# Own tiles transposed once and rescaled by a row on VectorE; the other tiles' statistics as running sums on ScalarE

## The reference

```python
xn = (x - mean) / sqrt(var + 1e-5)
# attention branch, per channel a decaying sum over earlier tokens
xm  = xn * time_mix + shift_one_token(xn) * (1 - time_mix)
k   = exp(min(xm @ Wk.T, 60));  v = xm @ Wv.T;  r = xm @ Wr.T
out1 = (sigmoid(r) * decaying_sum(k * v) / (decaying_sum(k) + 1e-16)) @ Wo.T
# ffn branch: a second normalisation of xn, then a ternary matrix
z   = (xn - mean(xn)) * rsqrt(var(xn) + 1e-3) * gamma + beta
g   = max(abs(z))                 # over the whole input
out2 = clip(z * 128 / g, -128 + 1e-5, 128 - 1e-5) @ ternary(W) * scale(g)
y = x + out1 + out2
```

## Time and profile before

| | us |
|---|---|
| median of 3 runs (892.36 to 892.97) | 892.81 |
| profiled execution, its own time | 891.49 |
| span of its trace | 889.7 |
| PE busy in the span | 867.1 (97%) |
| DVE busy | 764.8 (86%) |
| ACT busy | 510.3 (57%) |
| POOL busy | 215.2 (24%) |

### The profile page before, as it was taken

The page is one execution under the profiler, slowest core; times in us unless marked ns, Lnnn a source line. Parts: engine busy times, 40 slices in busy tenths (PEclk is TensorE's granted clock), DMA queues, the critical chain, the costliest instruction groups (busy, mean ns, idle before and its releaser), DMA issues.

```text
span 889.7 us, 12792 instructions
## 1 busy us (share of the span) xinstructions
PE 867.1 (97%) x3984; PEld 714.5 (80%) x3984; DVE 764.8 (86%) x1278; ACT 510.3 (57%) x834; POOL 215.2 (24%) x242
## 2 busy tenths in 40 slices
PE   3989999999999999999999999999999999999998
PEld 2778888888888888888888888888888888888886
DVE  5998999989897999989897897878978888789684
ACT  5584767667594757566564554545546536365441
POOL 5552326242452425240030100200201103011000
PEclk9999999999999999999999999999999999999999
DMA  8222415041423224045643245324451443424311
GB/s 283 108 83 88 149 54 184 13 171 54 165 71 135 101 82 154 12 172 136 212 145 115 84 154 189 125 75 141 153 175 57 157 141 96 154 93 142 95 48 47
DMA packets 59841, 107.13 MB, mean 120 GB/s; under 512 B 7712, under 2 KB 7712, under 8 KB 59808
## 3 DMA queue, kind: packets, MB, share of 16 engines
q1 hardware_dynamic: 59808, 106.73, 35.1%
HBM read 64.76 MB, written 41.96 MB: 120 GB/s over the span
## 4 chain that ended last, share of the span: by engine, by line
PE 90%; DVE 3%; issue 2%; POOL 2%; ACT 1%; DMA 0%; SPq 0%; POOLq 0%; DVEq 0%; ACTq 0%
PE kvr L513 18%; PE kvr L515 18%; PE kvr L514 18%; PE out_banks L552 7%; PE out_banks L554 7%; PE out_banks L534 6%; PE out_banks L533 6%; PE out_banks L531 6%; PE transposed L466 2%; PE out_banks L466 2%; DVE bn_stats L842 1%; POOL normed L1174 1%; POOL own_stats L1156 1%; POOL own_stats L1157 1%; DMA x<-in_x 0%
## 5 line engine op out<-in xcount | busy, mean ns | idle before, releaser
L1247 POOL TENSOR_TENSOR evacuated<-normed,mix_over_ffn_row 128x512 f32<-128x512 f32 x28 | 49.0, 1751 | 339.0 <-DVE ffn_lo L922 339.0
L513 PE MATMUL kvr<-xm_hi,wk_hi 128*128 128x512 f32 x256 | 103.7, 405 | 2.6 <-DVE xm_lo L922 2.6
L513 PE MATMUL kvr<-xm_hi,wv_hi 128*128 128x512 f32 x256 | 102.9, 402 | 2.2 <-DVE wv_lo L927 1.3
L513 PE MATMUL kvr<-xm_hi,wr_hi 128*128 128x512 f32 x256 | 102.7, 401 | 0.0
L515 PE MATMUL kvr<-xm_hi,wk_lo 128*128 128x512 f32 x256 | 101.0, 395 | 0.0
L514 PE MATMUL kvr<-xm_lo,wk_hi 128*128 128x512 f32 x256 | 100.7, 394 | 0.0
L515 PE MATMUL kvr<-xm_hi,wv_lo 128*128 128x512 f32 x256 | 100.2, 391 | 0.0
L515 PE MATMUL kvr<-xm_hi,wr_lo 128*128 128x512 f32 x256 | 100.1, 391 | 0.0
L531 PE MATMUL out_banks<-wo_hi,rwkv_hi 128*128 128x512 f32 x256 | 100.0, 390 | 0.0
L534 PE MATMUL out_banks<-wo_hi,rwkv_lo 128*128 128x512 f32 x256 | 99.7, 389 | 0.0
L514 PE MATMUL kvr<-xm_lo,wr_hi 128*128 128x512 f32 x256 | 99.7, 389 | 0.0
(11 more groups left out here) (140 smaller groups left out, 1922.7 us busy)
## 6 DMA issues: line engine op xcount, KB each, us to landing
other<-ffn_input SPq DMA_DIRECT2D x64, 256.0 KB, 5.1
x<-in_x SPq DMA_DIRECT2D x15, 1024.0 KB, 5.8
other<-in_x SPq DMA_DIRECT2D x8, 1024.0 KB, 5.8
ffn_input<-evacuated SPq DMA_DIRECT2D x32, 256.0 KB, 4.4
ffn_input<-parked SPq DMA_DIRECT2D x32, 256.0 KB, 2.2
attn_scratch<-x SPq DMA_DIRECT2D x8, 1024.0 KB, 4.2
parked<-attn_scratch SPq DMA_DIRECT2D x8, 1024.0 KB, 6.7
out<-parked SPq DMA_DIRECT2D x8, 1024.0 KB, 5.2
```

The source lines that it names most:

```text
L513: nc.tensor.matmul(KVR[:, m, :], hi, XH[t][:, ch, :], start=(ch == 0), stop=False)
L1247: G.tensor_tensor(U[:, n % RING, :], XN[:, ch, :], BC[:, :], ALU.mult).then_inc(pool_v, 1)
```

## The change

- **Own tiles.** Slots ffn_own0 and ffn_own1 become virtual: PE transposes nothing for them. When ACT evacuates a mix slot it first copies the transposed chunk as it is into a new buffer Y. The second normalisation differs from the first only by a factor per token, rsqrt(var(xn) + 1e-3). POOL computes this factor for the 512 tokens (`ratio`, 128x4); PE spreads it by four transposes of a broadcast column into a row that is equal in all partitions (`ratio_row`, after groups 9 and 21, and once at the start); ACT copies that to `RROW`; DVE multiplies the chunk of Y by it (`own_ffn_input`: in groups 10, 11 and twice in 12 for own1, and four after the last low part of a batch for the next own0). ACT then evacuates the virtual slot from Y instead of PSUM.
- **Own normalisations.** ACT's and POOL's second normalisation of own tiles goes, and with it two small POOL steps of nine.
- **Other tiles.** Except for the first one, mean and variance no longer come from bn_stats. ACT makes them as sums: for each of four 128-token blocks an Identity and a Square activation of (x - first channel) with an accumulated output (`other_sums`), after rwkv_hi of chunk 3 in group 12, and after the last high parts of a batch. POOL turns the sums into the variance with five more small operations.
- **Banks and waits.** The first four transposes go to OUT instead of TB and KVR; the wait for attn banks in `slot` moves from slots 1 and 14 to 5 and 16.

```diff
+ROW_AFTER = {9: 1, 21: 0}
...
+            def ratio_row(k, t, bank):
+
+
+                pe.wait_ge(pool_ratio, k + 1)
+                for q in range(Q):
+                    last = nc.tensor.transpose(bank[:, q * P:(q + 1) * P],
+                                               ratio[:, t, q:q + 1].to_broadcast([P, P]), ident[:, :])
+                last.then_inc(pe_row, 1)
...
-                    if ph == "B":
+                    if ph == "B" or n is not None and is_virtual(n):
                         n = None
...
+                    if ph == "A" and g in ROW_AFTER:
+                        t = ROW_AFTER[g]
+                        pe.wait_ge(dve_out, bank_use(b, ph, f"attn{1 - t}") + 1)
+                        ratio_row(2 * b + 2 - t, t, OUT[:, 0, :])
...
+                virtual = ph == "A" and is_virtual(n)
+                if virtual:
+                    act.wait_ge(dve_z, virtual_before(b, n) + 1)
...
+                        nc.scalar.activation(Y[:, ch, :], bank, ACT.Copy)
                         nc.scalar.activation(U[:, r, :], bank, ACT.Copy, scale=tmx[:, ch:ch + 1])
...
+            def other_sums(b, t):
+
+
+                act.wait_ge(s_oth, 32 * b + 16 * t + 16)
+                for q in range(Q):
+                    for i, func in enumerate((ACT.Identity, ACT.Square)):
+                        act.wait_ge(act_osum, CREDIT + 2 * Q * (2 * b + t - 1) + 2 * q + i - 1)
+                        nc.scalar.activation(UNUSED[:, i, :], ZA[:, q, :], func, bias=ZA[:, q, 0:1], scale=-1.0,
+                                             accum_out=osum[:, i, q:q + 1]).then_inc(act_osum, 1)
...
+            def own_ffn_input(b, n):
+
+                kind, ch = SLOTS[n]
+                t = int(kind[-1])
+                dve.wait_ge(act_row, 2 * b + t + 1)
...
+                V.tensor_tensor(Y[:, ch, :], Y[:, ch, :], RROW[:, t, :], ALU.mult).then_inc(dve_z, 1)
...
+            OWN_FFN_AT = {10: [12], 11: [13], 12: [14, 15]}
...
-                                if ph == "A":
-                                    tile_stats(b, ph, "other1", is_last)
...
+                if ph == "A" and not last_a:
+                    for ch in range(CH):
+                        own_ffn_input(b + 1, ch)
                 add_out(b, ph, "attn1")
                 if ph == "A" and not last_a:
-                    tile_stats(b + 1, ph, "other0", is_last)
                     largest(b)
```

More of the change, by code:

```diff
@@ L221, in slots_before, with is_virtual, pe_slots_before, virtual_before @@
             return n if ph == "P" else CH + len(SLOTS) * b + n
+        def is_virtual(n):
+            return SLOTS[n][0].startswith("ffn_own")
+        def pe_slots_before(b, ph, n):
+            if ph == "P":
+                return n
+            per_batch = sum(not is_virtual(k) for k in range(len(SLOTS)))
+            return CH + per_batch * b + sum(not is_virtual(k) for k in range(n))
+        def virtual_before(b, n):
+            return 2 * CH * b + sum(is_virtual(k) for k in range(n))
         def ffn_stores_before(b, n):
@@ L251, in normed_count @@
             if ph == "A":
-                return 4 * b + [k for k in SLOT_KINDS if "other" not in k].index(kind) + 1
-            return 4 * HALF + 2 * (b - HALF) + ["mix_own1", "mix_next0"].index(kind) + 1
+                return 2 * b + ["mix_own1", "mix_next0"].index(kind) + 1
+            return 2 * HALF
         def stats_number(b, ph, tile):
@@ L260, in stats_place, with dve_stats_before @@
         def stats_place(ph, tile):
-            return stats_number(0 if ph == "A" else HALF, ph, tile) % 2
+            return ["own1", "next0"].index(tile)
+        def dve_stats_before(b, tile):
+            return 2 * b + 2 + ["own1", "next0"].index(tile)
         def steps_before(i, ph):
@@ L288, in shifted @@
             return E[:, n % 2, :] if ph == "P" and n > 1 else WS[:, n % 2, :]
-        first_banks = [TB[:, :]] + [KVR[:, i, :] for i in range(3)]
+        first_banks = [OUT[:, q, :] for q in range(Q)]
         def slot_bank(ph, n):
@@ L593, in _, with copy_row @@
             act.sem_inc(act_r, CREDIT)
+            act.sem_inc(act_osum, CREDIT)
+            def copy_row(k, t, bank):
+                act.wait_ge(pe_row, 2 + k + 1)
+                nc.scalar.activation(RROW[:, t, :], bank, ACT.Copy).then_inc(act_row, 1)
             def evacuate(b, ph, n):
@@ L624, in evacuate @@
                         nc.scalar.activation(PLAIN[:, ch, :], bank, ACT.Copy)
-                    nc.scalar.activation(U[:, r, :], bank, ACT.Identity, bias=bet[:, ch:ch + 1],
+                    nc.scalar.activation(U[:, r, :], Y[:, ch, :] if virtual else bank, ACT.Identity,
+                                         bias=bet[:, ch:ch + 1],
                                          scale=gam[:, ch:ch + 1]).then_inc(act_u, 1)
@@ L707, in _ @@
                 high_part(0, "P", m)
[L708 to L712, removed]
             weight_hi("r")
+            for ch in range(CH):
+                last = nc.scalar.activation(Y[:, ch, :], first_banks[ch], ACT.Copy)
+            last.then_inc(act_first, 1)
+            copy_row(0, 0, TB[:, :])
             act.wait_ge(dve_w, 3 * CH)
@@ L800, in batch @@
                         high_part(b, ph, n)
+                    if not last_a:
+                        other_sums(b + 1, 0)
                 if last_a:
@@ L1121, in scales @@
                 dve.wait_ge(dve_s, 5)
-            tile_stats(0, "A", "other0", False)
+            dve.wait_ge(s_oth, 16)
+            stats_of(1, 1, ZA, 1, "A")
             weight_lo("o")
+            for ch in range(CH):
+                own_ffn_input(0, ch)
             with dve.Fori(0, HALF - 1) as b:
@@ L1196, in mix_call @@
             def mix_call(b, ph, tile):
[L1197 to L1208 removed]
+                return dve_stats_before(b, tile), stats_number(b, ph, tile), ph, stats_place(ph, tile)
@@ L1252, in batch_b @@
                         mix_input(b, n)
-            other(0, "other0")
+            other(0, "other0", first=True)
             with pool.Fori(0, HALF - 1) as b:
```

142 lines of the change are left out of this document (84 added, 58 removed).

## The result

The changed kernel takes 905.98 us (median of 4 runs, 905.76 to 907.14), the kernel before, timed beside it, 892.59; the ratio is 1.0154, 95% interval 1.0141 to 1.0168. Forecast were 895.2 us and a range up to 903.5. The sign was right, the size was not. The profiled execution took 906.11 us, its span is 904.3, 14.6 more than before.

A forecast was written before the change was run, and what follows sets the result against it. Phase A was taken as bound by PE. Batch 0 with the start +3.0 and batches 1 to 3 at -0.3 each gave +2.1 on 892.8: 894.9, rounded up to 895.2 us; range 886.5 to 903.5.

The forecast's parts named there:

- What PE saves: Phase A: 32 slots' transposes removed, 9 rows of four added; net 23 x 0.44 = 10.1 us if PE never waits anew.
- The start, +2.1: Ahead of batch 0's loop: four DVE multiplications delay exp of chunk 0, PE waits some 3.9 us; net +2.1, bounds 0 and +4.
- The wait for DVE in group 7: In the start: PE would wait for DVE in group 7 as before, 2.4 us later than now.
- rival 3: PE's pause in the start lowers its clock; at worst 2 us more, 897; chance: the rest after 46%, 30% and 21%.
- T to slot 8, 24.65: From a batch's first slot to mix_own1's first: 25.85 falls to 24.65, range 23.8 to 25.6; gain 1.2 us.
- Slot 8 to slot 20: Two stretches, split at the output product's end: 26.93 to 27.8 (+0.9 us), then 22.41 to 22.0 (gain 0.4).
- both stalls: PE waits 0.9 us for rwkv_lo in the output product's fourth part, and 0.9 for POOL at slot 16.
- Rival 1: Idle DVE and ACT catch up, PE waits only in the start: 886.1 us, between 884 and 891; chance 30%.
- Rival 2: ACT's accumulated sums are slower than plain activations, 0.1 to 0.25 us each or twice that: 901 to 909; chance 21%.
- The sum: Phase A: batch 0 +3.0, batches 1 to 3 -0.3 each, together +2.1 us; phase B unchanged.
- the 0.3 of rounding: 894.9 us rounded up to 895.2 for the clock after PE's pause in the start.

The follow-up runs named there:

- add_ahead: Changed kernel with DVE adding the output product to own1 before it multiplies the next own0 by its row; 898.35 us, ratio 1.0059.
- stores_ahead: Changed kernel with only SP's queue reordered: stores of slots 0 to 2 of the next batch issued before own1's store wait and load; 897.48 us.
- slot13: stores_ahead with DVE multiplying slot 13's chunk two groups later, together with those of slots 14 and 15; 897.29 us, ratio 1.0036.
- split_sums: slot13 with half of the middle sums moved into ACT's idleness ahead of chunk 3's logarithm; 890.74 us, ratio 0.9974.
- sums_alone: Kernel before with the other tiles' sums on ACT instead of bn_stats on DVE, own tiles as before; 893.38 us, ratio 1.0006.
- pool_wo: stores_ahead with wo_lo made by POOL instead of DVE in the start; 896.97 us, ratio 1.0043.

## Why the prediction was wrong, point by point

- *What PE saves.* Right: 92 instructions less, and no stretch shows another price than 0.44 us for a slot's transposes.
- *The start, +2.1.* Slot 8 of batch 0 is at 55.02, +2.71. The step is right in kind (exp at 34.56, PE waits 2.80 for it instead of 3.9; slot 8 waits 2.12), the size within its bounds. The wait for DVE in group 7 did not come, and the clock fell behind the pause, which was in rival 3 alone; that the number comes near is partly luck.
- *T to slot 8, 24.65.* This is the step that failed, and it is one sentence: "That is cover used up, not yet a wait." The forecast saw that add_out ends 2.5 us later and that "store and load of that tile follow it". It did not go on along SP's queue to the stores of slots 0 to 3, which stand behind that load, nor to ACT, which needs slot 0's buffer again at slot 4. Those 2.0 to 2.1 us, in batches 1 to 3, are 6.1. add_ahead and stores_ahead take them away by two unlike edits and win 7.6 and 8.5 us: in their traces this stretch is 5.6 and 6.7 us shorter in the three batches together, and the 1.5 of the clock in batch 3 is gone too. With ACT's wait gone the stretch is 24.75 and 24.29 in batch 2, by the size that the other steps of that paragraph gave it.
- *Slot 8 to slot 20.* Right to 0.3 us in sum in batch 2 (50.06 against 49.8), and both stalls are where they were put. But they are links of one chain: slot13 shows that to free rwkv_lo alone lengthens the wait at slot 16, split_sums that this one goes too when, besides, half the sums come earlier. Without slot13's edit that was not run.
- *Rival 1* failed: the slack of DVE and ACT was not where it was needed. *Rival 2* is refuted as a mechanism, though the time fell on its side: a sum is an ACTIVATE of 0.71 and a read of the accumulator of 0.19 that overlaps it, and the next begins 0.70 to 0.71 later; eight take 5.65 us, estimated were 5.6. *Rival 3* was right about the start (clock 0.61 behind the pause, with a wait for POOL left at slot 8); it did not see the same loss behind slot 8, 1.5 us in batches 0 and 3.
- *The sum.* Of the 12.5 us missing in the span (14.6 - 2.1), 6.1 are the first stretch, 3.0 the clock behind slot 8, which the sum held at nothing (the 0.3 of rounding was for the start), and 0.6 the start. About 2.8 are left: 0.4 a batch between slot 8 and the end of the output product, 1.2 in all from there to the next batch, the rest in phase B; they are not assigned to a cause.

## What to carry to other kernels

When a step moves back on one engine, follow what is queued behind its DMA, not its DMA alone: on a queue that takes things in order, a late store makes late whatever stands behind it, and a ring of four buffers turns that into a wait four slots on. A stall that is removed shows first what was hidden behind it; follow the chain on to the next link (here the sums, moved into idleness ahead of them) before the edit is judged.

## What the runs showed of the hardware

The pauses of ACT come in those passes of its loop that are entered by a jump back (batches 1 and 2): none in stores_ahead, 3.8 us a pass with 16 more instructions ahead of the loop, and with them 11 packets more on the queue of the kind "instruction". That the place of the loop in the code decides is the reading that fits; the place itself was not varied. The Trainium skill (Runtime: NRT & Kernel Launch, Instruction fetch mechanics) says that a taken branch to code outside the two pages held has to fetch it first. The rows agree in place and kind; which code was missing no run here shows.

POOL's subtraction took 6.65 us and held DVE's beside it to 6.14 instead of 2.49. The Trainium skill (SBUF — State Buffer, Who interferes with whom) has the two engines share a pair of ports under an exclusive lock; the rows agree.

What makes the clock fall behind slot 8 is open. In the changed kernel it fell after 2.12 us of waiting in batch 0 and 2.20 in batch 3, not after 1.93 in batch 2. In sums_alone it fell after 2.16, and in pool_wo it stayed up after 2.16 (55.94, the next slot at 59.16), as in the kernel before after 2.13. So the length of the wait alone does not decide.
